# Four convolution taps on VectorE for batches 0 to 2, the plain inner projection on TensorE

## The reference, cut to what matters

```
xr = layernorm(x) @ W_in                      # 128 -> 512 channels
xi, res = split(xr)                           # 256 inner channels, 256 gate channels
xc[c, t] = sum over j of conv_w[c, j] * xi[c, t - 3 + j]  + conv_b[c]     # 4 taps, causal, one filter per channel
u = silu(xc);  gate = silu(res)
dbc = u @ W_x                                 # step size, B and C of the state loop
delta = softplus(dbc[:8] @ W_dt + b_dt)
h = exp(delta * A) * h + delta * B * u;  y = C . h      # over 128 tokens, 16 states
y = (y + u * D) * gate;  x = x + y @ W_out
```

## Time and profile before

| what | value |
|---|---|
| time before, median of 3 runs | 268.65 us (266.66, 268.65 and 321.47) |
| profiled execution, span | 261.7 us; a whole time for this execution isn't listed |
| lowest and middle run less that span | 4.96 and 6.95 us |
| mean granted TensorE clock | 0.936 of full speed |
| PE / DVE / ACT / POOL busy | 206.7 / 195.9 / 162.4 / 63.9 us |

### The profile page before, as it was taken

The page is one execution under the profiler, slowest core; times in us unless marked ns, Lnnn a source line. Parts: engine busy times, 40 slices in busy tenths (PEclk is TensorE's granted clock), DMA queues, the critical chain, the costliest instruction groups (busy, mean ns, idle before and its releaser), DMA issues.

```text
span 261.7 us, 4957 instructions
## 1 busy us (share of the span) xinstructions
PE 206.7 (79%) x1629; PEld 147.4 (56%) x1631; DVE 195.9 (75%) x567; ACT 162.4 (62%) x539; POOL 63.9 (24%) x73
## 2 busy tenths in 40 slices
PE   7797898898898788888927577999996699986213
PEld 4676786676864333443413345867785588964002
DVE  5468659764089999999787785687667599996776
ACT  3686749433795689898267755144426779984422
POOL 6012200053017788888920010000001000001000
PEclk9999999999979999999986999999999889999555
DMA  6999900000001888200000042000000000000001
GB/s 221 431 395 419 404 26 3 1 3 0 3 0 17 92 93 93 27 3 0 1 0 1 0 112 51 0 3 0 0 3 3 3 0 1 3 1 3 1 0 40
DMA packets 6745, 16.06 MB, mean 61 GB/s; under 512 B 320, under 2 KB 5056, under 8 KB 5696
## 3 DMA queue, kind: packets, MB, share of 16 engines
q1 hardware_dynamic: 6432, 15.62, 20.8%
q10 hardware_dynamic: 288, 0.13, 0.2%
HBM read 13.39 MB, written 2.35 MB: 60 GB/s over the span
## 4 chain that ended last, share of the span: by engine, by line
PE 38%; DVE 23%; ACT 18%; issue 10%; POOL 7%; another core or an unknown queue 2%; DMA 1%; DVEq 0%; POOLq 0%; ACTq 0%
PE bank L1189 32%; POOL region L420 6%; ACT probs L513 4%; DVE region L983 3%; PE bank L1608 3%; DVE region L853 3%; DVE region L807 2%; ACT region L612 2%; PE bank L1291 2%; ACT k_groups L455 1%; DMA early_sb<-early 1%; DVE region L796 1%; ACT region L580 1%; DVE bank L964 1%
## 5 line engine op out<-in xcount | busy, mean ns | idle before, releaser
L420 POOL TENSOR_TENSOR region<-region 128x512 f32<-128x512 f32 x31 | 39.1, 1273 | 9.0 <-DVE region L983 8.1
L1189 PE MATMUL bank<-k_groups,region 128*128 128x128 f32 x256 | 36.1, 287 | 4.1 <-ACT k_groups L455 2.9
L983 DVE TENSOR_TENSOR_SCAN region<-region,bank 128x512 f32<-128x512 f32 x32 | 37.9, 1209 | 1.5 <-PE bank L1460 1.4
L1189 PEld LDWEIGHTS bank<-k_groups,region 128*128 128x128 f32 x256 | 32.2, 198 | 6.9 <-ACT k_groups L455 3.7
L1189 PE MATMUL bank<-region,early_sb 128*128 128x512 f32 x64 | 31.8, 599 | 1.4 <-POOL region L420 1.2
L513 ACT ACTIVATE probs<-bank,neg_max 128x128 f32<-128x128 f32 x64 | 22.6, 365 | 12.0 <-DVE neg_max L848 11.8
L386 POOL TENSOR_TENSOR xb<-x,rows_sb 128x512 f32<-128x512 f32 x3 | 3.8, 1264 | 105.9 <-ACT x L715 44.1
L513 ACT ACTIVATE probs<-region,neg_max 128x128 f32<-128x128 f32 x64 | 24.9, 390 | 5.6 <-DVE neg_max L853 5.4
L1189 PE MATMUL bank<-ctx_T_sb,region 128*32 128x128 f32 (+1 forms) x288 | 25.0, 312 | 2.0 <-DVE v_heads L764 1.6
L807 DVE COPY region<-bank 128x512 f32<-128x512 f32 x32 | 21.9, 685 | 3.9 <-PE bank L1291 3.9
L439 ACT ACTIVATE lnv<-mv,eps_col 128x1 f32<-128x1 f32 x24 | 7.0, 292 | 28.3 <-DVE mv L753 26.9
(11 more groups left out here) (214 smaller groups left out, 429.4 us busy)
## 6 DMA issues: line engine op xcount, KB each, us to landing
ctx_sb<-ctx SPq DMA_DIRECT2D x4, 1024.0 KB, 24.9
ctx_T_sb<-ctx_T SPq DMA_DIRECT2D x3, 1024.0 KB, 10.1
late_sb<-late SPq DMA_DIRECT2D x1, 2416.0 KB, 18.7
bias_scratch<-bias_vec SPq DMA_DIRECT2D x1, 2040.0 KB, 24.7
ctx_T_sb<-ctx_T SPq DMA_DIRECT2D x2, 512.0 KB, 5.7
region<-bias_scratch SPq DMA_DIRECT2D x1, 1024.0 KB, 5.7
early_sb<-early SPq DMA_DIRECT2D x1, 512.0 KB, 3.5
region<-taps SPq DMA_DIRECT2D x1, 512.0 KB, 19.4
```

The lines of the kernel that those rows point to most:

```text
L420: done(pool.tensor_tensor(read[:, k % 3, :], state[:, k % 3, :], c_sb[:, n % 2, :], ALU.mult), "read")
L983: done(dve.tensor_tensor_scan(state[:, k % 3, :], decay[:, k % NDA, :], bank[3 + k % 3][:, :], 0.0, ALU.mult, ALU.add), "state")
L1189: return pe.matmul(dst, lhsT, rhs, start=start, stop=stop)
```

## The change

For groups 0 and 1 PE makes the plain projection `xi` (two matmuls a group), and DVE reads it four times from PSUM, multiplies each time by a tap column and sums into `u`; ACT takes SiLU in place from `u`. Group 2 stays as it was. The tap columns come from a new small DMA (8 rows of 128), a matmul with the identity in `weight_sums`, and a copy by DVE. The projection of group 0 stands at t=18, its gates move from t=23 to t=20, the projection of group 1 stands at t=22 ahead of `proj`, and the gates of group 1 move behind the steps, to bank 4.

```
-CHANNELS = {17: [(0, 0)], 18: [(0, 1)], 23: [(0, "gates"), (1, "gates")], 25: [(1, 0), (1, 1)]}
+CHANNELS = {18: [(0, "inputs")], 20: [(0, "gates")], 22: [(1, "inputs")]}
+CONVOLVE = {18: (0, 3), 19: (0, 1), 22: (1, 3), 23: (1, 1)}
...
+            sp_.dma_start(tap_rows, taps.rearrange("(r p) -> r p", p=P)).then_inc(S["tap_rows_in"], 16)
...  (ACT)
+                if i < LAST_GROUP:
+                    act.wait_ge(S["conv_sb"], i + 1)
+                    for hf in range(DH):
+                        cols = slice(b0 * P, b1 * P)
+                        done(act.activation(u[:, hf, cols], u[:, hf, cols], ACT.Silu, bias=C("conv_b", hf)), "u")
+                    return
...
-                act.wait_ge(S["gates_ps"], i + 1)
+                act.wait_ge(S["gates_ps"], len(SSM_GROUPS) if i else 1)
...
             gates(0)
+            channel_inputs(2)
             gates(1)
-            channel_inputs(2)
             gates(2)
...  (DVE)
+                done(dve.tensor_copy(tap_cols[:, :], bank[6][:, 16:16 + CONV * DH]), "tap_cols")
...
+            def convolve(i, first):
+                b0, b1, conv_at, _ = SSM_GROUPS[i]
+                n = (b1 - b0) * P
+                if first == CONV - 1:
+                    dve.wait_ge(S["tap_cols"], 1)
+                    dve.wait_ge(S["xi_ps"], i + 1)
+                for j in (first, first - 1):
+                    lag = CONV - 1 - j
+                    for hf in range(DH):
+                        at, col = conv_at[hf]
+                        src = bank[at][:, col:col + n].rearrange("p (b t) -> p b t", b=b1 - b0)
+                        dst = u[:, hf, b0 * P:b1 * P].rearrange("p (b t) -> p b t", b=b1 - b0)
+                        if lag:
+                            after(conv_at_step[hf])
+                            ins = dve.scalar_tensor_tensor(dst[:, :, lag:], src[:, :, 0:P - lag], tap_cols[:, j * DH + hf:j * DH + hf + 1],
+                                                           dst[:, :, lag:], ALU.mult, ALU.add)
+                        else:
+                            ins = dve.tensor_scalar(dst, src, tap_cols[:, j * DH + hf:j * DH + hf + 1], None, ALU.mult)
+                        if j == 0 and hf == DH - 1:
+                            done(ins, "conv_sb")
+                        else:
+                            conv_at_step[hf] = mark(ins)
...  (end of each step t of DVE's attention)
+                    if ph == 0 and t in CONVOLVE:
+                        convolve(*CONVOLVE[t])
...  (PE, weight_sums)
+                pe.wait_ge(S["tap_rows_in"], 16)
+                mm(bank[6][:, 16:16 + CONV * DH], tap_rows, ident[0:CONV * DH, 0:CONV * DH])
...  (PE, channels)
+                if part == "inputs":
+                    for hf, (at, col) in enumerate(conv_at):
+                        ins = mm(bank[at][:, col:col + n], L("w_in")[:, hf * P:hf * P + P], xn_pad[:, b0:b1, CONV - 1:])
+                    done(ins, "xi_ps")
+                    return
...  (PE, after the steps)
-            for part in (0, 1, "gates"):
-                channels(2, part)
+            for group, part in ((2, 0), (2, 1), (1, "gates"), (2, "gates")):
+                channels(group, part)
```

More of the change, by code:

```diff
@@ L76 @@
 LAST_TURN, LAST_QK = 2, 6
-CHANNELS = {17: [(0, 0)], 18: [(0, 1)], 23: [(0, "gates"), (1, "gates")], 25: [(1, 0), (1, 1)]}
+CHANNELS = {18: [(0, "inputs")], 20: [(0, "gates")], 22: [(1, "inputs")]}
+CONVOLVE = {18: (0, 3), 19: (0, 1), 22: (1, 3), 23: (1, 1)}
 FILLS = {"early_in": 20, "bc_parts": 16, "hidden": 12, "hidden_rest": 12, "swiglu_out": 4}
-SSM_GROUPS = [(0, 2, [(0, 0), (0, 2 * P)], (1, 0)), (2, 3, [(2, 0), (2, P)], (2, 2 * P)),
+SSM_GROUPS = [(0, 2, [(0, 0), (0, 2 * P)], (1, 0)), (2, 3, [(2, 0), (2, P)], (4, 2 * P)),
               (3, 4, [(3, 0), (5, 0)], (4, 0))]
+LAST_GROUP = len(SSM_GROUPS) - 1
 def places(fields):
@@ L212, in two_layers @@
         b_tok = sb("b_tok", [P, NB, NS])
+        tap_cols = sb("tap_cols", [P, CONV * DH])
         w_red = sb("w_red", [P, 5])
@@ L218, in two_layers @@
         w_tmp = sb("w_tmp", [P, INNER])
+        tap_rows = w_tmp[0:CONV * DH, 0:P]
         q_heads = turn("heads", [HG, T], at=8960)
@@ L308, in v_tok_at @@
             return bank[6 if v else 4][:, 2 * P:3 * P]
-        names = """taps_in early_in cols_in late_in rows_in bias_out bias_in stored consts ones_set eps_set act_step dve_step
+        names = """taps_in tap_rows_in tap_cols xi_ps conv_sb early_in cols_in late_in rows_in bias_out bias_in stored consts ones_set eps_set act_step dve_step
             pool_step w_red w_diag w_all w_scaled w_quant bias_vec bias_sb ln_mv ln_rstd xn xnT xnT_sb x_ready
@@ L468, in channel_inputs @@
                 n = (b1 - b0) * P
+                if i < LAST_GROUP:
[4 more added lines that the diff above has]
+                    return
                 for hf in range(DH):
                     shared = conv_at[0][0] == conv_at[1][0]
-                    act.wait_ge(S["conv_ps"], DH * i + (DH if shared else hf + 1))
+                    act.wait_ge(S["conv_ps"], DH if shared else hf + 1)
                     at, col = conv_at[hf]
@@ L832, in token_extremes @@
                 done(dve.tensor_reduce(ext[:, 0, 1, b:b + 1], xn[:, b, :], AX, ALU.min, negate=True), "ext")
+            conv_at_step = {}
+            def convolve(i, first):
[20 more added lines that the diff above has]
+                            conv_at_step[hf] = mark(ins)
             def attention(ph):
```

## The result

| | median, us | runs, us | ratio to the kernel before |
|---|---|---|---|
| changed kernel, first sitting | 269.35 | 268.22 to 270.92 (4) | 1.015 [1.009, 1.021] |
| the same code, second sitting | 270.54 | 268.56 to 273.11 (4) | 1.023 [1.013, 1.033] |

The ratios leave out executions that stand over 1.5% above the lowest of their kernel, so they are not quotients of the medians. The kernel before ran in 266.66 to 268.65 us in the first sitting (and once in 321.47), and with a median of 265.93 in the second. So the change makes the kernel slower, by 1.5 to 2.3%; on which side of 2% it lies, the intervals leave open. 270.1 us was forecast: the time is met within 0.8 us.

The account below looks back on a forecast made before the run. PE's list bounds two pieces, 4 and 5.9 us; between them the path changes hands, DVE's list on it too. +1.43 and +1.0 make +2.4, a span of 264.1; with 6.0 around it 270.1 us, range 266.4 to 273.2.

Parts of the forecast that it names:

- Step 1: In `weight_sums`, two tiny PE passes and one small DVE copy: +0.25 us, between 0 and 0.64.
- Step 2: Group 0's projection: 2.6 us of PE goes, four taps take 1.60; add of batch 2 starts 0.96 us earlier.
- Step 3: Group 0's other four taps, ahead of `normed` of batch 2: the gain is gone, `normed` 0.14 us later.
- Step 4: Group 1's projection and four taps stand ahead of the add of batch 3, which starts 1.63 us later.
- Steps 5 and 6: SiLU table load hides the last taps; then 36 passes, not 48, wait for batch 3's copy: `dbc` +1.43 us.
- Step 7: PE idles before the 36 passes, so its clock falls: 1.4 us, bounds 0 and 1.65; net +1.0.
- Something comes back: Behind `dbc`, an earlier clock fall may remove DVE's 0.39 us wait for `b_tok`; net +1.0, between -0.4 and +1.65.
- Around the span: Time of a run above its profiled span: 6.0 us, the middle of 4.96 and 6.95 from two undisturbed runs.
- hidden taps: Rival: taps hide in DVE's idle time ahead of batch 2's add, not slower; best 266.6 us; chance 0.17.
- dear taps: Rival: taps ahead of both adds and both `normed` cost more, 275.3 us at twice the price; over 2% slower; chance 0.06.
- the clock stays up: Rival: no clock fall in PE's gap before the 36 passes; 269.1 us; chance 0.25.
- falls in later layers: Clock falls in later layers that shift with the start of this one; chance 0.05.

Follow-up runs that it names:

- taps_out: Changed kernel with all DVE taps left out but one column per group, so no convolution is computed, the waits for the projections kept; 264.65 us (one run).
- group1_late: Changed kernel with group 1's projection moved behind batch 3's projection and its taps behind batch 3's moments; 267.46 us, 1.009 of the kernel before.
- fill_gap: Changed kernel plus 24 matmuls on ones in PE's gap ahead of batch 3's last turn; 268.64 us, 1.007 of the kernel before.
- group1_late_fill: Changed kernel with group 1's projection and taps moved later, plus 11 matmuls on ones ahead of the last turn; 266.99 us, 0.998 of before.
- all_late_copy: Changed kernel with all taps behind the last normalisation, ACT's gates and `skip` first, SiLU table load behind batch 3's copy; 265.14 us, 0.999 of before.
- before_order: Kernel before, no taps on DVE, group 0's convolution halves moved behind the projections of batches 2 and 3 on PE; 265.17 us, 0.997 of before.

## Why the prediction was right in direction and too small

- **Step 1** (+0.25): 0.32 measured, the 0.73 at the add of batch 1 less the 0.41 of the start. Right.
- **Step 2** (0.96 gained, 1.60 of taps eating the rest): from add 1 to add 2, 6.97 became 5.80. That is 1.17 gained; 6.97 - 0.96 - 0.25 of step 1 gives 5.76. taps_out shows the eaten part, 1.26.
- **Step 3** (`normed` of batch 2 later by 0.14, step 1's 0.25 in it, so 0.11 earlier behind add 1): 8.28 us after add 1 against 8.40, 0.12 earlier. Right.
- **Step 4** (+1.63 at add 3): from add 1 to add 3, 9.87 became 11.22, +1.35, and 1.63 - 0.25 is 1.38. Between adds 2 and 3 alone it is 5.42 - 2.90 = 2.52, of which group1_late takes 1.84 away by order alone.
- **Steps 5 and 6** (+1.43 at `dbc`, 1.18 of it behind add 1): fill_gap, with the clock up, has 18.97 - 17.83 = 1.14. Right.
- **Step 7**, the fall itself (1.4, at most 1.65): 1.34 in the first profiled execution; in the second the stretch is 21.36 - 18.97 = 2.39 longer than with the clock up, beyond my bound, because the grant stayed low for 6.8 us there and 3.4 in the first. The rule of the Trainium skill, TensorE: Matmul & The Clock Gate, "HAM oscillation — how this bites in real kernels", that matmuls behind a long wait begin at the low clock, agrees here: grants of 0.76 and 0.59 behind 3.06 us of idling, 1.00 with the gap filled. The wait's length by itself does not decide, though: the clock fell behind 1.15 and 0.88 us in group1_late, and did not behind 2.04 and 0.88 in taps_out.
- **The term that failed** is in step 7: "Something comes back", net +1.0. In the first execution the opposite came: the clock was low again from 78.0, `b_tok`'s wait grew from 0.39 to 1.58 (+1.20 at the loop's second read), and two later layers lost 1.07 and 1.68 us. I priced one fall, in its own stretch, and put everything behind it at nothing. In the second execution 0.46 did come back at the loop's start, and 1.64 was lost in the SwiGLU. So behind `dt_low` the changed kernel paid 4.2 and 0.9 us more than before, where I took -0.4. From add 1 to the last operation that makes 6.66 us (212.70 against 206.04) and 4.46 (210.50), where step 6's 1.18 and step 7's net 1.0 make 2.2. The rise of over 3 us that I had named as a sign of something unseen came in the first execution only.
- **Around the span** I took 6.0 us; all four runs of the first sitting show 1.8. These 4.2 too many covered the clock's missing share, so that by luck the time in us came out within 0.8 although the ratio was too low. The listed runs of before were simply longer executions than the profiled one, and I took the difference for an offset.
- **The range** has a wrong sum: with step 1 at its end, the full fall and 7 us around the span its upper end is 261.7 + 1.43 + 0.39 + 1.65 + 7 = 272.2, not 273.2. The measured 269.35 and 270.54 lie inside either.

The rivals: hidden taps fell with taps_out; dear taps fell by 0.39 and 0.26 us a tap. That the clock stays up is refuted by both profiled executions of the changed kernel. The 0.05 that I gave to falls in later layers was the case that came, with the forecast's own mechanism ahead of it.

Open is why the clock falls in the later layers in some executions and not in others. The work there is the same, and no experiment held it apart: low grants came at 153.1 and 166.7 in the first execution of the changed kernel, at 151.7 in the second, in neither place in group1_late_fill. They also come without a fall in the stretch: fill_gap, at full clock there, took 4.53 us from the first to the last add of the SwiGLU (low grant from 149.8), against 3.16 before, and all_late_copy, also at full clock there, had a wait of 1.60 us for `b_tok`. So what the change adds behind `dt_low`, and what is scatter from execution to execution, is not shown; the listed executions of before themselves lie between 263.75 and 269.17 us, the one of 321.47 apart.

## What to carry to other kernels

Work that moves to an engine with idle time still stands in that engine's list: ahead of an operation on the path it can cost much of its length, and the wait for its own input besides. Here twelve taps stand ahead of the second add; they last 4.2 us and cost 2.07 there. Behind the adds, or singly in the waits, the same taps went with a time 0.6 to 0.7% below before. How much of that is order alone is not shown by the times: before_order, without any tap, stands at 0.997, and the intervals overlap. In the stretch the two versions with taps are shorter than before_order by 1.0 and 2.0 us.

When work leaves TensorE, look for the idle stretch that it leaves and price the fall of the clock behind it, as a range: the same code lost 1.34 us to it in one execution and 2.39 in another. Later stages can lose to a low clock too, here up to 1.7 us each, with or without a fall in the stretch that was changed, so a forecast of a whole time needs a range for them as well.

## What the runs showed of the hardware

- The start of the kernel is not fixed. The add of batch 1 stands between 53.3 and 55.8 us in executions whose code is alike up to there but for step 1; the trace's record of the granted clock begins, at full speed, at 6.1 us in before, 9.7 in after and 13.6 in group1_late, and matmuls ahead of that are slower: the 8 passes of `k_groups` near 10 us take 1.16 us in after and 2.07 in group1_late. In before_order, the one with 55.8, the grant was 0.50 from 8.1 to 14.9. That is up to 2.4 us of scatter, as much as this change was forecast to do, so intervals from a mark inside the kernel told more than times: add 1 to add 2 is 5.80 in five executions of four kernels.
- A tap that reads PSUM and accumulates in place in SBUF takes 0.86 us for two, started 0.39 apart, at 254 of 256 columns: adding in place costs nothing beside the plain product of the first tap (0.88 for two).
